# Scatter-adds of a routed mixture of experts: two in flight, ordered between experts by a table of counts

## What is computed

```python
x = x + tanh(g_xattn[0]) * xattn(ctx_512, layernorm(x), W, b)      # 4 x 512 x 512
h = layernorm(x).reshape(-1, 512)
probs = softmax(h @ gate_w.T)                                       # 16 experts
vals, idx = top_k(probs, 4); w = vals / sum(vals)
combine = einsum('tke,tk->te', one_hot(idx, 16), w)
act = swiglu(einsum('th,ehi->eti', h, dequant_fp4(gate_up)))
y_e = einsum('eti,eih->eth', act, dequant_fp4(down))
out = einsum('te,eth->th', combine, y_e) + shared_expert(h)
x = x + tanh(g_ffn[0]) * out
```

## Time and profile before

| | |
|---|---|
| three runs | 731.17, 736.95, 737.34 us; median 736.95 |
| profiled execution | 733.4 us |
| its span, first to last instruction | 731.6 us |
| mean granted TensorE clock | 0.94 of full speed |
| TensorE / VectorE / ScalarE / POOL busy | 631.8 / 525.2 / 316.9 / 319.1 us |
| matmuls and transposes | 4586 |
| DMA | 93.73 MB, 128 GB/s over the span |

### The profile page before, as it was taken

One profiled execution on the slowest core, in us unless ns is written; L12 is line 12 of the kernel. 1 busy time (PEld: TensorE's weight loads), 2 busy tenths in 40 slices (PEclk: granted clock), 3 DMA queues, 4 the chain that ended last, 5 costly groups with the idle time before them and its releaser, 6 DMA issues.

```text
span 731.6 us, 17952 instructions
## 1 busy us (share of the span) xinstructions
PE 631.8 (86%) x4586; PEld 387.6 (53%) x4587; DVE 525.2 (72%) x1299; ACT 316.9 (43%) x542; POOL 319.1 (44%) x504
## 2 busy tenths in 40 slices
PE   4112769999999699999999999999999999899992
PEld 3012445666656366556555565555555555565660
DVE  5999778877598586768887867688678888767210
ACT  2333573222234345455444454554444554445441
POOL 1464620000113454546456455554656455465532
PEclk9655769999999899999999999999999999999997
DMA  7661135110216679485866866767585776655432
GB/s 226 214 185 50 68 102 138 59 58 2 73 31 174 148 170 185 90 205 99 187 146 140 205 126 153 164 126 185 118 172 120 174 190 113 167 96 98 83 48 39
DMA packets 48524, 93.73 MB, mean 128 GB/s; under 512 B 7677, under 2 KB 15339, under 8 KB 48498
## 3 DMA queue, kind: packets, MB, share of 16 engines
q0 software_dynamic: 16128, 38.35, 29.6%
q1 hardware_dynamic: 32370, 55.07, 25.2%
HBM read 65.16 MB, written 28.24 MB: 128 GB/s over the span
## 4 chain that ended last, share of the span: by engine, by line
DMA 48%; PE 27%; DVE 10%; POOL 5%; issue 4%; ACT 2%; POOLq 2%; SPq 1%; DVEq 0%; ACTq 0%
DMA out<-mix_room,idx_s 46%; PE gu_ps L1113 15%; PE bank L1140 6%; DVE stats L671 2%; PE bank L1166 2%; POOL idx_s L480 2%; POOL pool_tick L458 2%; PE bank L1127 1%; DMA room_b<-token_rows,idx_g 1%; POOL mix_room L410 1%; POOLq L462 1%; DVE wgu L872 1%; PE bank L1152 1%; DMA out<-X 1%; ACT xT L532 1%
## 5 line engine op out<-in xcount | busy, mean ns | idle before, releaser
L1113 PE MATMUL gu_ps<-wgu,mix_room 128*128 x1728 | 305.4, 327 | 1.7 <-DVE tick L895 1.7
L1113 PEld LDWEIGHTS gu_ps<-wgu,mix_room 128*128 128x128 f16 x1728 | 166.4, 98 | 113.1 <-issue 8.0
L1140 PE MATMUL bank<-wdn,aT 128*128 (+1 forms) x792 | 186.1, 380 | 1.4 <-ACT aT L570 1.0
L570 ACT ACTIVATE aT<-bank 128x768 f16<-128x768 f16 x88 | 71.3, 810 | 144.1 <-PE bank L1127 137.1
L483 POOL DMA_INDIRECT out<-mix_room,idx_s x72 | 120.2, 1669 | 19.3 <-issue 19.1
L1140 PEld LDWEIGHTS bank<-wdn,aT 128*128 128x128 f16 x792 | 77.7, 98 | 86.6 <-issue 4.2
L939 DVE SCALAR_TENSOR_TENSOR act<-gu_ps,wslot,sg x72 | 44.5, 618 | 93.9 <-ACT sg L556 82.8
L467 POOL COPY idx_g<-room_b 128x1 int32 x72 | 56.1, 780 | 120.0 <-issue 100.1
L480 POOL COPY idx_s<-room_b 128x1 int32 x72 | 16.6, 230 | 192.1 <-DMA out<-mix_room,idx_s 164.3
L563 ACT ACTIVATE acth<-act 128x384 f16<-128x384 f32 x88 | 46.0, 523 | 120.6 <-DVE act L939 111.0
L470 POOL DMA_INDIRECT room_b<-token_rows,idx_g x72 | 78.1, 1084 | 11.2 <-issue 1.7
(11 more groups left out here) (156 smaller groups left out, 665.1 us busy)
## 6 DMA issues: line engine op xcount, KB each, us to landing
dn_sc<-dn_scale_halves SPq DMA_DIRECT2D x34, 384.0 KB
dn_raw<-in_L_ffn_down_packed SPq DMA_DIRECT2D x48, 256.0 KB
gu_sc<-gu_scale_halves SPq DMA_DIRECT2D x34, 192.0 KB
X<-in_x SPq DMA_DIRECT2D x4, 1024.0 KB, 11.6
token_rows<-room_a SPq DMA_DIRECT2D x16, 256.0 KB, 2.1
out<-X SPq DMA_DIRECT2D x4, 1024.0 KB, 4.5
gu_raw<-in_L_ffn_gate_up_packed SPq DMA_DIRECT2D x16, 192.0 KB
gu_raw<-in_L_ffn_gate_up_packed SPq DMA_DIRECT2D x16, 191.9 KB
```

Source lines behind the costliest of these rows:

```text
L570: nc.scalar.activation(aT[:, b].rearrange("p a c t -> p (a c t)"), at_ps, ACT.Copy).then_inc(aT_done, 1)
L1113: mm = nc.tensor.matmul(ps[b][:, 0:I], x(xp * HC + c), wgu[:, w, wp, c, col:col + I], start=(c == 0 and xp == 0 and wp == 0), stop=(c == H ...
L1140: mm = nc.tensor.matmul(y_ps[b][:, :], aT[:, b, ap, t, :], wdn[:, w, wp, t, :], start=(n == 0), stop=(n == 3 * IC - 1))
```

## The change

Two semaphores `added[0]` and `added[1]`, one per buffer, take the place of `added`. A scatter waits for the last one of its own buffer (s - 2), and for the other buffer up to a count that is read from a new table, `slot_i[:, 2, s]`: 16 times the number of slots of the other parity that belong to earlier experts, at least 16. The table is made by four new steps in `slot_tables(3)`, from the sum that this part works out in any case (the first slot of the slot's expert) and a row of 0, 1, 0, 1 that POOL writes at the start. The last scatter waits for all before it. ScalarE's wait for the buffer of y names the semaphore of that buffer.

```diff
--- before.py
+++ after.py
@@ -195,8 +195,9 @@
         TILES_ROOM = 2 * KMAX
         first_tiles_i = sb("first_tiles_i", [P, E], I32)
         pairs_i = sb("pairs_i", [P, 1], I32)
-        slot_f = sb("slot_f", [P, 2, SLOTS], F32)
-        slot_i = sb("slot_i", [P, 2, SLOTS], I32)
+        slot_f = sb("slot_f", [P, 3, SLOTS], F32)
+        slot_i = sb("slot_i", [P, 3, SLOTS], I32)
+        odd_s = sb("odd_s", [P, SLOTS], F32)
         iota_s = sb("iota_s", [P, SLOTS], F32)
         idx_g = sb("idx_g", [P, 2], I32)
         idx_s = sb("idx_s", [P, 2], I32)
@@ -281,7 +282,7 @@
         xTs_done = sem("xTs_done")
         wslot_done = sem("wslot_done")
         yev_done = sem("yev_done")
-        added = sem("added")
+        added = [sem("added0"), sem("added1")]
         idx_g_ready = sem("idx_g_ready")
         idx_s_ready = sem("idx_s_ready")
 
@@ -311,7 +312,7 @@
 
             return 16 * LOADS * (n // 2 + 1)
 
-        POOL_CONST = 14
+        POOL_CONST = 15
         SPLIT_STEPS = 10
 
         @block.sync
@@ -384,10 +385,10 @@
             nc.gpsimd.memset(tri[:, :], 1.0).then_inc(pool_const, 1)
             nc.gpsimd.memset(ones16[:, :], 1.0).then_inc(pool_const, 1)
             for dst, pattern, base, mult in ((token1[:, :], [[P, NT]], 1, 1), (dump_row[:, :], [[0, 1]], DUMP + 1, 1),
-                                             (iota_s[:, :], [[1, SLOTS]], 0, 0)):
+                                             (iota_s[:, :], [[1, SLOTS]], 0, 0), (odd_s[:, :], [[0, SLOTS // 2], [1, 2]], 0, 0)):
                 nc.gpsimd.iota(dst, pattern, base=base, channel_multiplier=mult,
                                allow_small_or_imprecise_dtypes=True).then_inc(pool_const, 1)
-            pool.wait_ge(pool_const, 11)
+            pool.wait_ge(pool_const, 12)
 
             nc.gpsimd.affine_select(out=tri[:, :], in_=tri[:, :], compare_op=ALU.is_gt, fill=0.0, base=0,
                                     pattern=[[1, P]], channel_multiplier=-1).then_inc(pool_const, 1)
@@ -470,18 +471,23 @@
                 nc.gpsimd.indirect_dma_start(xg[:, b, :], None, rows_dram[:, :],
                                              bass.IndirectOffsetOnAxis(idx_g[:, b:b + 1], 0)).then_inc(xg_ld[b], 16)
 
-            def add(s, b):
+            def add(s, b, all_before=False):
 
                 col = pool.value_load(slot_i[0:1, 1, bass.ds(s, 1)], min_val=0, max_val=E * KMAX)
                 pool.wait_ge(yev_done, s + 1)
+                if not isinstance(s, int) or s >= 2:
+                    pool.wait_ge(added[b], 8 * (s - b))
                 if not isinstance(s, int) or s >= 1:
-                    pool.wait_ge(added, 16 * s)
+                    others = pool.value_load(slot_i[0:1, 2, bass.ds(s, 1)], min_val=16, max_val=8 * SLOTS)
+                    pool.wait_ge(added[1 - b], others)
+                if all_before:
+                    pool.wait_ge(added[1 - b], 8 * (s + b))
                 pool.wait_ge(st_out, 16 * (B + 1))
                 nc.gpsimd.tensor_copy(idx_s[:, b:b + 1], tok[:, bass.ds(col, 1)]).then_inc(idx_s_ready, 1)
                 pool.wait_ge(idx_s_ready, s + 1)
                 hold_wait()
                 nc.gpsimd.indirect_dma_start(out[:, :], bass.IndirectOffsetOnAxis(idx_s[:, b:b + 1], 0), y_sb[:, b, :],
-                                             None, compute_op=ALU.add).then_inc(added, 16)
+                                             None, compute_op=ALU.add).then_inc(added[b], 16)
             for s in range(4):
                 gather(s, s % 2)
             for b in range(2):
@@ -492,8 +498,9 @@
                     gather(2 * j + b + 2, b)
                     add(2 * j + b - 2, b)
             for k in range(-4, 0):
-                add(2 * inner + 4 + k, k % 2)
-            pool.wait_ge(added, 32 * inner + 64)
+                add(2 * inner + 4 + k, k % 2, all_before=k == -1)
+            for b in range(2):
+                pool.wait_ge(added[b], 16 * inner + 32)
 
         @block.scalar
         def _(a):
@@ -583,7 +590,7 @@
             def take_y(r, b):
                 a.wait_ge(y_done, NT + r + 1)
                 if not isinstance(r, int) or r >= 2:
-                    a.wait_ge(added, 16 * (r - 1))
+                    a.wait_ge(added[b], 8 * (r - b))
                 nc.scalar.activation(y_sb[:, b, :], y_ps[b][:, :], ACT.Copy, scale=1.0 / W_SCALE).then_inc(yev_done, 1)
 
 
@@ -798,6 +805,10 @@
                     step(nc.vector.tensor_copy(slot_i[:, 0, :], slot_f[:, 0, :]), wait=False)
                 else:
                     step(nc.vector.tensor_reduce(slot_f[:, 1, :], slot_nt, AX, ALU.add))
+                    step(nc.vector.tensor_tensor(slot_f[:, 2, :], slot_f[:, 1, :], odd_s[:, :], ALU.add))
+                    step(nc.vector.tensor_scalar(slot_i[:, 2, :], slot_f[:, 2, :], 8.0, None, ALU.mult))
+                    step(nc.vector.tensor_scalar(slot_i[:, 2, :], slot_i[:, 2, :], 0xFFF0, None, ALU.bitwise_and))
+                    step(nc.vector.tensor_scalar(slot_i[:, 2, :], slot_i[:, 2, :], 16, None, ALU.max))
                     step(nc.vector.scalar_tensor_tensor(slot_f[:, 1, :], slot_f[:, 0, :], float(KMAX), slot_f[:, 1, :],
                                                         ALU.mult, ALU.subtract))
                     step(nc.vector.tensor_tensor(slot_i[:, 1, :], slot_f[:, 1, :], iota_s[:, :], ALU.add))
```

## The result

The changed kernel takes 725.32 us (median of 5 runs, 724.08 to 728.89), the kernel before 736.95 in the runs beside it: a ratio of 0.986 (95% interval 0.982 to 0.990; the two medians alone would give 0.984). On two other chips the same kernel gave 0.990 (0.986 to 0.994) and 0.990 (0.987 to 0.993).

What follows compares the result with a forecast made beforehand. It took scatter chain and TensorE to run neck and neck, with late gathered rows as the main loss. Terms -9.4 + 2.0 + 0.5 = -6.9 us, taken from the runs' mean of 735.2, gave 728 us, range 719 to 738.

Steps and rivals of the forecast that it cites:

- What comes back: Third to last tick, 58 slots: without gather waits, experts at their size's best price take 391.2 against 400.56 us, -9.4 us.
- rival A: In the routed stage, VectorE's lateness goes too: up to 16 us go, 1 to 2 return, 720 us; chance 0.20.
- The waits that stay: At an expert's first, still serial scatter: one late gather in each of two runs of four-slot experts gives back 2.0 us.
- POOL's extra load: Register load between the wait for y and the scatter: 0.5 us, hidden in POOL's 5.4 us round, costing +0.5 us at the end.
- VectorE's table steps: Four new steps making the table, about 1.2 us, hidden in VectorE's 1.57 us of idle time waiting for ScalarE.
- The start unchanged: The routed stage's first four slots, 239 to 273 us, would still take 33.93 us.
- rival C: Two scatters beside a weight load stretch it, so VectorE waits at L890 in several experts: 767 or 748 us; chance 0.09.
- Rival B: Gathers stay late in the queue shared with scatters and weight loads, L1152 waiting near 10 us: 733 to 736 us; chance 0.23.
- What bounds the kernel: Long stretch of the routed stage: 16 us lost above TensorE's 6.63 us a slot, 10.8 of them waits for late gathered rows.
- Neck and neck: Scatter chain against TensorE: a usual scatter repeats in about 5.9 us, below TensorE's 6.63; only slow ones push the chain above.
- What would show it: Signs: L1152 waits shrink to two or three, POOL's idle laid to ScalarE, scatters 2.1 us after y, stretch some 393 us.

Runs made afterwards that it cites:

- e4: Changed kernel with odd slots' scatters sent to a second tensor, so no scatter waits for one of the other buffer: 725.65 us, ratio 0.991 to the kernel before.
- e1: The changed kernel itself, run once more without any edit: 725.81 us.
- e8: Changed kernel with three more register loads of the table in every scatter, between y and the issue: 738.95 us, ratio 1.004 to the kernel before.
- e3: Kernel before, scatters still strictly serial, each gather issued ahead of the scatter it stood behind: 732.67 us, ratio 0.999 to the kernel before.
- e10: Kernel before, taking the next expert's words after the fourth slot's product and issuing the third routed expert's loads ahead of out's last store: 735.28 us, ratio 0.999.

## Why the prediction was right or wrong

Its forecast was 728 us, 719 to 738, from a change of -6.9 us; 725.32 came, and between like executions the change is -7.8 and -8.7. By its own steps:

- **What comes back, -9.4.** Right. The price by the best expert of each size, 391.2 us for the stretch, met 391.64 and 391.40. That VectorE's lateness would stay, so that four-slot experts take 27.5 and not 26.5, was right too; rival A fell.
- **The waits that stay, +2.0.** Mis-sized: it is 0. The serial step was foreseen, at 9.9 + 1.1 = 11.0 us, and came, at 9.9 (383.68 to 393.58), but no gather waits anywhere in the list. The step took POOL's round as 5.4 us and its catching up as 1 us a slot. The round is 4.9 with the new load in it, since a register load and its work run while POOL is still busy with the instruction ahead. POOL catches up by 1.7 us a slot. e4 shows that nothing is left to gain there. About 1 us in e1, ahead of the third tick, which the sum didn't have, hides part of the error; it is no more than these stretches vary by (the first expert: 33.5, 34.6 and 33.9 us in three executions).
- **POOL's extra load, hidden, +0.5 at the end.** Right in kind: the end, from the last tick to the end of the span, went from 57.8 us to 58.6 (e1: 58.5), 0.7 to 0.8, the issue coming 2.25 us after the last y but one starts instead of 1.61 (716.59 - 714.98). The 0.5 us for a load stands against this 0.64 and the 0.54 of e8. The end of cover was put at a round of 6.7 us; e8's own round was 5.9 to 6.3 and it lost time all the same, so the cover ends earlier than a comparison of rounds says, where the queue has lateness to work off. The Trainium skill (DMA: Bandwidth & Descriptors, Latency and other measured facts) gives a register load a floor of about 600 ns. The load of the table takes 0.29 us at the median in the trace after, which doesn't agree.
- **VectorE's table steps, 1.2 us, hidden.** Right: four steps of 0.24, 0.20, 0.20 and 0.20 us, 0.98 us with their gaps, and the idle time behind them went from 1.57 to 0.60:

```profile
159.72 0.24 DVE L808 TENSOR_TENSOR slot_f<-slot_f,odd_s 128x80 f32<-128x80 f32 x1
...
161.83 0.62 DVE L950 SCALAR_TENSOR_TENSOR act<-gu_ps,shared_w,sg 128x384 f32<-128x384 f32 x1 [0.60 <-ACT sg L563]
```

- **The start unchanged.** Right within a microsecond: 33.53 and 34.59 against 33.93 us. With that, rival C fell: no second expert waits for its loads. Rival B fell as well: the gathers, issued earlier, came in time beside loads and two scatters.
- **What bounds the kernel.** This is the reading that failed though the number stood. The prediction took 10.8 us of waits for gathered rows as the loss and asked why a gather is late. e3 takes all these waits away and gains nothing; in e10 they are longer (16.4 us) with TensorE's better start. The loss was the difference between the chain's 7.00 us a slot and what the other engines need, 6.74, and it shows at TensorE or ScalarE, whichever stands behind POOL. "Neck and neck" was an understatement that came from pricing a usual scatter at 5.9 us and one slow one per expert on top, without dividing the chain by its slots: that one division names the bound, and the price of what is next gives the most that can be gained. Both roads lead to the same sum here because the change loosens the chain itself. To that extent the number was luck: by the same reading e3, which moves the gathers alone, was thought able to bring as much.
- **What would show it.** The stretch of some 393 us was 391.6; where nothing holds them scatters follow y by 2.2 to 2.6 us instead of 2.1; the L1152 waits went to none, not two or three. POOL's idle time went to ScalarE only in part (57.2 us, against 111.6 for scatters): at an expert's start it still waits, 5 us and more at a time, at no cost.

## What to carry to other kernels

A chain's share of the span (48% here) says who came last, not what it costs: divide the chain by its rounds and compare with the price of a round for whoever is next; here 7.00 against 6.74 us. That is the most there is to gain, and not the gain: over 48 slots it would be 12 us, and the stretch gave 9, since the same slots run at 6.82 to 6.85 after. A wait found behind an in-order queue names a neighbour of the cause; an experiment that moves only the neighbour (e3) tells the two apart before a rewrite is made. Order DMAs by what they touch: within an expert the rows are disjoint, and a serial step at the seams was free because the queue could catch up (1.7 us a slot); with 0.3 to 0.8 (e8) time was lost, though the queue's round still fitted into a slot.

## What the runs showed of the hardware that had not been expected

**The start at half rate.** TensorE's score products (L1088) are four pairs. The first and second in the profiled execution of the changed kernel, then in that of e1_after, which is the same program:

```profile
13.21 1.92 PE L1088 MATMUL gu_ps<-room_b,wj_all 128*128 128x512 f32 x2
...
16.49 2.05 PE L1088 MATMUL gu_ps<-room_b,wj_all 128*128 128x512 f32 x2
```

```profile
12.45 1.92 PE L1088 MATMUL gu_ps<-room_b,wj_all 128*128 128x512 f32 x2
...
15.39 1.10 PE L1088 MATMUL gu_ps<-room_b,wj_all 128*128 128x512 f32 x2
```

The first pair is slow in both. From the second on, the same two instructions take 1.9 times as long in the one as in the other, about what 1.2 GHz instead of 2.4 would give, while the granted clock of this stretch is shown as 1.00 in both. Around 50 us the clock's column differs (changed kernel, then e1_after), though the first transposes after the pause take the same:

```profile
50.00:60.00 10.00, 3.59 (x40) 2.99 (x40) 9.72 (x22) 4.37 (x7) 4.55 (x4) 1.00 0.22 82
```

```profile
50.00:60.00 10.00, 3.84 (x48) 3.36 (x48) 9.22 (x19) 5.62 (x9) 5.19 (x5) 0.50 0.25 92
```

```profile
52.33 1.02 PE L1108 MATMUL bank<-id,room_a 128*128 128x128 f16 x8 [25.11 <-DVE room_a L711]
```

```profile
47.83 1.02 PE L1108 MATMUL bank<-id,room_a 128*128 128x128 f16 x8 [26.68 <-DVE room_a L711]
```

So here the rows of durations tell the rate and the clock's column does not, and for the same reason the mean clock of the whole execution comes out higher in such executions (0.98 against 0.94), not lower. What decides which executions begin so is not known, and a second profiled execution of this sort (e4_two_targets) shows the same slow pairs.

**Register loads run ahead.** With two register loads in it POOL's round is 4.9 us, below the 5.4 of its parts laid end to end: only 0.20 us of idle time is left between the gather's instruction and the copy that both loads stand before (396.14 + 1.03 to 397.37). Three more in a row, behind the wait for y, cost 0.54 us each (2.25 to 3.87 us from y to the scatter).

**A scatter beside weight loads.** An accumulating scatter of 128 rows lands 4.6 to 5.0 us after its issue as a rule and up to 9.9 beside weight loads, and two in flight left these numbers alone (least, median, most: 4.7, 5.0 and 9.7 us against 4.6, 4.9 and 9.9).
